# A Mamba layer with a mixture of experts on one core: the state norm in two parts, the carry between the products, XN one step earlier

## The reference

```python
var = mean(x*x, -1); xn = x * rsqrt(var + 1e-6) * norm_w
x_branch, gate = split(xn @ W_in.T)
xc = silu(conv4(x_branch) + conv_b)
dt = soft_clamp(softplus(xc @ W_dt.T + b_dt), 0.001, 0.1, 0.5)
dA = exp(soft_clamp(dt * A, -8, 8, 0.5)); dB = dt * (xc @ W_B.T); C = xc @ W_C.T
def step(h, t):                       # h is 8 x 512 x 16
    h = h * dA[t] + dB[t] * xc[t]
    nrm = sqrt(sum(h * h))            # over 512 x 16, per batch
    if t % 10 == 0: h = h * min(20 / (nrm + 1e-8), 1)
    y[t] = sum_n(h * C[t]) + D * xc[t]
out = (y * silu(gate)) @ W_out.T
```

## Time and profile before

| | before |
|---|---|
| median of 3 runs | 2973.71 us (2963.92 to 2985.89) |
| the profiled execution | 2959.9 us, its span 2958.1 us |
| TensorE (PE) busy | 2648.4 us, 90% |
| its weight loads (PEld) | 2381.6 us, 81% |
| VectorE (DVE) busy | 2488.2 us, 84% |
| ScalarE (ACT) busy | 2265.4 us, 77% |
| GpSimd (POOL) busy | 2165.0 us, 73% |
| granted TensorE clock, mean | 0.968 |

### The profile page before, as it was taken

One profiled execution on the slowest core, in us unless ns is written; L12 is line 12 of the kernel. 1 busy time (PEld: TensorE's weight loads), 2 busy tenths in 40 slices (PEclk: granted clock), 3 DMA queues, 4 the chain that ended last, 5 costly groups with the idle time before them and its releaser, 6 DMA issues. The chain is left out here.

```text
span 2958.1 us, 50935 instructions
## 1 busy us (share of the span) xinstructions
PE 2648.4 (90%) x16400; PEld 2381.6 (81%) x16400; DVE 2488.2 (84%) x3452; ACT 2265.4 (77%) x5161; POOL 2165.0 (73%) x2239
## 2 busy tenths in 40 slices
PE   4899999999999999999999999999999874899992
PEld 4888888888888898888888988888888774667762
DVE  1999999999999999999999999999999996112123
ACT  6999899899898898988989999989899831111113
POOL 1788888888888888888888888888888872334215
PEclk8999999999999999999999999999999986999996
DMA  2222222222222222222222222222222222134226
GB/s 64 64 71 74 76 67 79 73 70 79 69 77 77 67 79 70 73 76 71 77 74 66 79 73 74 77 71 76 75 65 81 66 61 88 42 90 100 56 45 238
DMA packets 153969, 225.67 MB, mean 76 GB/s; under 512 B 46056, under 2 KB 92776, under 8 KB 152552
## 3 DMA queue, kind: packets, MB, share of 16 engines
q1 hardware_dynamic: 131208, 188.98, 22.1%
q0 software_dynamic: 9216, 12.59, 2.4%
q10 hardware_dynamic: 13280, 20.86, 2.1%
HBM read 189.26 MB, written 33.05 MB: 75 GB/s over the span
## 5 line engine op out<-in xcount | busy, mean ns | idle before, releaser
L642 POOL TENSOR_TENSOR H<-H,CB 128x640 f32<-128x640 f32 x832 | 1262.9, 1526 | 273.9 <-DVE H L479 268.3
L479 DVE TENSOR_TENSOR_SCAN H<-DA,PM 128x704 f32<-128x704 f32 x832 | 1320.8, 1608 | 20.8 <-ACT DA L276 1.2
L394 ACT ACTIVATE DA<-DT,SM 128x160 f32<-128x160 f32 x3328 | 1115.9, 425 | 1.6 <-POOL DT L610 0.3
L664 PE MATMUL YB<-H,ID 128*128 128x160 f32 x6656 | 1049.2, 310 | 0.5 <-POOL H L642 0.5
L664 PEld LDWEIGHTS YB<-H,ID 128*128 128x128 f32 x6656 | 987.8, 191 | 16.7 <-issue 11.2
L454 DVE TENSOR_TENSOR PM<-PM,BB 128x640 f32<-128x640 f32 x832 | 642.3, 817 | 5.1 <-issue 0.4
L276 ACT ACTIVATE DA<-DA 128x2560 f32<-128x2560 f32 x208 | 485.3, 2334 | 1.6
L1119 POOL DMA_INDIRECT YA<-YS,IG x48 | 75.2, 1566 | 239.7 <-ACT YS L942 228.1
L628 POOL TENSOR_TENSOR FC<-SN,HALF 128x4 f32<-128x4 f32 x206 | 212.4, 1031 | 47.8 <-DVE SN L485 35.3
L670 PE MATMUL PA<-XN,WIN 128*128 128x160 f32 x832 | 153.8, 332 | 58.5 <-POOL XN L622 57.0
L763 PE MATMUL PZ<-WO,Z 128*80 128x256 f32 x832 | 188.2, 379 | 0.1
(11 more groups left out here) (164 smaller groups left out, 3654.0 us busy)
## 6 DMA issues: line engine op xcount, KB each, us to landing
BB<-Bd SPq DMA_DIRECT2D x208, 320.0 KB, 3.5
CB<-Cd SPq DMA_DIRECT2D x208, 320.0 KB, 3.4
W<-in_w ACTq DMA_DIRECT2D x16, 1024.0 KB, 7.5
XT<-in_xT SPq DMA_DIRECT2D x52, 160.0 KB, 2.2
XR<-in_xp SPq DMA_DIRECT2D x416, 20.0 KB
X2d<-VV SPq DMA_DIRECT2D x416, 20.0 KB
YA<-VV SPq DMA_DIRECT2D x416, 20.0 KB
HI<-YA SPq DMA_DIRECT2D x6, 1024.0 KB, 9.9
```

Source lines behind the costliest of these rows:

```text
L394: eng.activation(DA[:, c0:c0 + 2, :, a, m, 1:11].rearrange("p c b t -> p b c t"), DT[:, j % 2, a].rearrange("p b (c t) -> p b c t", c=2), ...
L479: eng.tensor_tensor_scan(H[:, q % 3, u], a0, DBX(u), 0.0, ALU.mult, ALU.add).then_inc(s_scan, 1)
L642: eng.tensor_tensor(h, h, cb, ALU.mult).then_inc(s_hc, 1)
L664: mm = eng.matmul(yv, ID[:], hv[:, :, :, n, 0:10], start=False, stop=n == 15)
```

## The change

Three edits.

1. The norm matmul is issued as two of 128 columns that accumulate in the same 128 columns of PSUM: the first over states 0 to 31 of each batch row's 64 columns of SQ, the second over 32 to 63. `NP`, its output, is half as wide, and `norm_sum` reduces 32 columns for each batch row instead of 64.
2. On VectorE `carry(q, u)` stands between `mult(q, u)` and `mult(q, u + 1)` instead of behind both.
3. On GpSimd XN is written at step 14, behind CAR and ahead of that step's H*C, instead of at step 15.

```diff
--- before.py
+++ after.py
@@ -130,7 +130,7 @@
             return YB[q % 2][:, 0:160]
 
         def NP(q):
-            return YB[1 - q % 2][:, 256:512]
+            return YB[1 - q % 2][:, 256:384]
 
 
         def two(j):
@@ -520,8 +520,8 @@
                                 ALU.add, ALU.mult).then_inc(s_xc, 1)
                     if live and u % 2 == 0:
                         mult(q, u)
+                        carry(q, u)
                         mult(q, u + 1)
-                        carry(q, u)
                     if u == 2 and 1 <= q <= NQ - 2:
                         norm_sum(q - 1)
                     if live:
@@ -614,13 +614,6 @@
                         if j >= 2:
                             eng.wait_ge(s_z, 4 * (j - 1))
                         eng.tensor_copy(SG[:, j % 2, :, :, 0:1], SG[:, 1 - j % 2, :, :, 20:21]).then_inc(s_sgh, 1)
-                    if s == 15 and ok(i + 3):
-                        j = i + 3
-                        eng.wait_ge(s_rs, j + 1)
-                        if j >= 2:
-                            eng.wait_ge(s_gt, 2 * (j - 1))
-                        eng.tensor_tensor(XN[:, j % 2], XT[:, j % 2], RST[:].unsqueeze(1).to_broadcast([128, 2, 160]),
-                                          ALU.mult).then_inc(s_xn, 1)
                     if u == 2 and 1 <= q <= NQ - 2:
 
                         p = q - 1
@@ -633,6 +626,13 @@
                         eng.tensor_tensor(CAR[:], H[:, p % 3].rearrange("p u (a t) -> p u a t", t=11)[:, :, :, 10],
                                           FC[:, p % 2].unsqueeze(2).to_broadcast([128, 4, 64]),
                                           ALU.mult).then_inc(s_car, 1)
+                    if s == 14 and ok(i + 3):
+                        j = i + 3
+                        eng.wait_ge(s_rs, j + 1)
+                        if j >= 2:
+                            eng.wait_ge(s_gt, 2 * (j - 1))
+                        eng.tensor_tensor(XN[:, j % 2], XT[:, j % 2], RST[:].unsqueeze(1).to_broadcast([128, 2, 160]),
+                                          ALU.mult).then_inc(s_xn, 1)
                     if live:
                         h = H[:, q % 3, u].rearrange("p (a n t) -> p a n t", a=4, n=16)[:, :, :, 0:10]
                         cb = CB[:, q % 2, :, u, :].unsqueeze(1).to_broadcast([128, 4, 16, 10])
@@ -702,7 +702,9 @@
                     if u == 0 and 1 <= q <= NQ - 2:
                         p = q - 1
                         eng.wait_ge(s_hsq, q)
-                        eng.matmul(NP(p), MEAN[:], SQ[:], start=True, stop=True).then_inc(s_nrm, 1)
+                        for a in range(2):
+                            mm = eng.matmul(NP(p), MEAN[:], SQ[:, :, 32 * a:32 * a + 32], start=a == 0, stop=a == 1)
+                        mm.then_inc(s_nrm, 1)
                     if u == 2:
                         y_sum(q - 1, 0, 6)
                     if u == 3:
```

## The result

| | before | after |
|---|---|---|
| median of the runs | 2977.74 us (4 runs, 2963.92 to 2985.89) | 2886.55 us (4 runs, 2885.02 to 2887.11) |
| the profiled execution | 2959.9 us | 2887.04 us |
| VectorE busy, 1000 to 1500 us | 493.05 us | 498.15 us |
| one iteration | 45.37 us | 44.07 us |

The changed kernel takes 0.9698 of the time before, with a 95% interval of 0.9659 to 0.9736. Between the two profiled executions 72.9 us went; the medians of the runs differ by 91, and the spread shrank from 22 us to 2. Both differences need an explanation: the first is the sum of the edits, the second most likely a matter of one instruction, the first `dt_x` of an iteration.

What follows compares the result with a forecast made beforehand. The prediction took VectorE's instruction stream as the bound; 37.4 + 26.8 + 4.2 + 4.6 = 73.0 us off the profiled 2959.9 gave 2886.9, and half of 13.8 added gave 2893.8, rounded to 2893, range 2870 to 2931.

Steps and rivals of the forecast that it cites:

- The bound: The loop's 52 iterations are VectorE's instruction stream laid end to end; a gain there shortens the loop.
- The carry: The second product covers the copy's end before the scan at u = 0: 208 slots x 0.18 = 37.4 us.
- Rival 2: The copy or the scan still waits 0.18 us somewhere in the new order: 2930 us, chance 0.11.
- The norm: VectorE's reduction reads 128 elements instead of 256: 0.13 us, 206 times, 26.8 us; nothing added on TensorE.
- Rival 4: TensorE or ScalarE becomes the bound, from slower 128-column passes or overlooked waits: 2903 to 2919 us, chance 0.09.
- XN: Earlier XN ends TensorE's 1.26 us idle before the projection; VectorE's ten XC waits, 4.2 us, are gained.
- whether the clock still falls or not: At VectorE's XC: the 4.2 us of waits are gained even if the granted clock still drops to 0.50.
- The race: At the first `dt_x` of an iteration: four losses to GpSimd's H*C end, 4 x 1.16 = 4.6 us.
- `dt_x` will come 0.06 us behind the start of XN and win each time: The norm sum, shorter by 0.13 us, brings the first `dt_x` forward, so it never waits for GpSimd: 4.6 us.
- Rival 3: The first `dt_x` loses to XN and waits 0.67 us, 52 times, 35 us: 2933 us, chance 0.10.
- Rivals 5 and 6: 5: the copy waits for CAR, slower, 3004 us, chance 0.02. 6: little effect, above 2944 us, chance 0.02.
- I keep half of the 13.8: The runs' median lay 13.8 us above the profiled execution; half was kept in the forecast: 2893.8, rounded to 2893.

Runs made afterwards that it cites:

- carry_only: The kernel before with only the copy of CAR moved between the two products: 2918.37 us, ratio 0.9854.
- pad_memset: The kernel before with a memset of 4 columns between the copy of CAR and the scan at u = 0: 2991.00 us, ratio 1.0001.
- pe_extra: The changed kernel with the norm's two matmuls issued twice in every second slot: 2887.84 us.
- no_xn: The kernel before with norm and carry changed and XN left at step 15: 2902.30 us, ratio 0.9798.
- norm_only: The kernel before with only the norm in two parts, reduced from 128 columns: 2933.85 us, ratio 0.9905.
- no_norm: The kernel before with the copy of CAR and XN moved, the norm as before: runs of 2911.88 to 2925.70 us.

## Why the prediction was right, and where it was not

- **The bound.** Right. VectorE's stream made the loop before and makes it after. The sum for the profiled execution was 2886.9 us; it took 2887.04. That it met the time to 0.1 us is partly luck: the terms were each off by 1 to 2 us or more, in both directions.
- **The carry.** Right in mechanism, slightly under in size: 0.19 us a slot, 39 us over 208, against 37.4. The scan at u = 0 also hands over 0.01 us sooner when it has not been held. CAR was never late; the changed kernel's waits of VectorE name no CAR. Rival 2 did not occur: 0.19 us follow every copy, in carry_only too. pad_memset shows that the 0.18 us can be filled.
- **The norm.** Right: 0.13 us, 26 us in all against 26.8. TensorE's price was 0.01 us a slot, as the line between the bounds had it, and pe_extra shows that even 0.9 us more of passes an iteration cost 1.3 us in all, within the runs' spread of 3 us. Rival 4 did not occur.
- **XN.** The cause was right and the account incomplete. The 4.2 us were the waits at the iteration's old length. The changed kernel keeps one of 1.9 us near the loop's start, at 136 us. In the faster iteration the same dips of the clock would have cost VectorE 14.6 us, as no_xn shows; the edit keeps the other two from paying for the clock. My sum came out right because it let both fall, without saying what the clock would cost if it did not rise: the step "whether the clock still falls or not" was wrong, since with the dips the gain would have been about 15 us smaller (no_xn is 15.8 above the changed kernel). Of the idle time that went, 0.62 us came back at the y sum, not 0.3, and for Z, not for H*C; it cost nothing.
- **The race.** The result was right, none lost, and in part by luck. The "four times at 1.16" were three of 1.15 at 0.19 us and one of 0.9 at 0.43 us, 4.4 us together; none of the four is left. The step "`dt_x` will come 0.06 us behind the start of XN and win each time" was not safe: with H*C in XN's place it loses one time in three there in one execution, and only the fact that XN stands there now, for a reason that stays open, has kept it from that. norm_only (one execution of five) and no_norm both lose races; the changed kernel and no_xn lose none after the loop's first iterations.
- **The other rivals.** Rival 3, a loss to XN in every iteration, did not come either, though no_norm shows it in 20 iterations at 0.53 us each, where I had put 0.67. Rivals 5 and 6 are excluded by the result.
- **The median.** The step that was off is "I keep half of the 13.8" (2893.8, which I rounded the wrong way). The runs of the kernel before lay above its profiled execution, most likely because of lost races, and the changed kernel has none, so all of it went: 2886.55 us instead of 2893. The reason had been given in the same paragraph, and the half was caution. Much of the 91 us between the medians is thus the state of the kernel before: beside the medians of 2961 us in two of the groups, 2886.55 is 74.5 to 75.2 us less.

## What to carry to other kernels

On a bounding engine, don't let an instruction wait on the one directly ahead of it: put anything that does not need the result in between, and the 0.18 us that a wait on a short copy cost here are hidden. Before a term is taken off the bounding engine, ask which side condition of the old pace hid a cost: here the edit that ended the drops of TensorE's clock was worth 6 us at the old pace and 16 at the new one. Where the runs of a kernel spread by 1% without a cause in the data, look for an instruction of two lengths: an operation of VectorE with two inputs in SBUF that starts within 0.3 us of one of GpSimd's. A single trace can miss it: compare the profiled execution's time with those of the other runs.

## What was not expected of the hardware

- Whether VectorE or GpSimd goes first, when `dt_x` starts 0.2 us after GpSimd's instruction, differs within one execution at the same distance (no_norm lost 20 and won 19 at 0.20 to 0.21 us). The times of the kernel before spread, most likely with it: 2959.01 to 2962.53 us twelve times on one chip, 2959.71 once and 2984 to 3000 thirteen times on another, 2959 to 2964 seven times and 2990.36 once on the third. Whether the chip, the moment or the execution decides stays open.
- In the traced executions `dt_x` loses about 0.07 us behind H*C in one kernel (norm_only) and from about 0.19 us up, and never at 0.05, 0.10 or 0.18. The cause of the first losing place stays open.
- A memset of 4 columns between the copy and the scan that waits on it took no time at all (start to start 0.37 us with it and without).
